# Moving a cross-partition sum of squares from TensorE to GpSimd, and packing a prefix count into fewer matmuls, in a fused scan and mixture-of-experts layer

## The chip, the cores and the metric

The kernel runs on one core of one Trainium2 chip. The metric is the device time of one execution in microseconds (us). The kernel before takes 681.78 us, the median of 3 runs (680.64 to 683.04). A difference of about 0.3% is what a measurement of this kernel can tell from none.

## What is computed

The reference, cut to what matters (8 sequences of 512 tokens, 256 features; 8 experts of 1024 hidden units, two chosen per token, and one shared expert that every token uses):

```python
xn = layernorm(x)
# scan branch
g, v, d = xn @ Wg + bg, xn @ Wv + bv, xn @ Wd + bd
a = 0.001 + 0.998 * sigmoid(d)
scan = linear_scan(sigmoid(g) * tanh(v), a)          # along each sequence
# expert branch, T = 4096 tokens
scores = sigmoid(xn @ Wgate.T + bg + bias)
weights = scores of the two best experts of a token, 0 for the others
h = gelu(einsum('td,ehd->teh', xn, W1) + b1)
combined = einsum('ted,te->td', einsum('teh,edh->ted', h, W2) + b2, weights)
shared = gelu(xn @ Ws1.T + bs1) @ Ws2.T + bs2
out = x + scan + shared + combined
```

## The kernel before, in words

All matrix products are done in float16 pairs: a float32 matrix is scaled by a power of two and split into a high and a low half, and three products (high by high, high by low, low by high) are added in PSUM. The scale of a weight matrix comes from the sum of its squares, so each of the nine weight sets (set 0 is the shared expert's, sets 1 to 8 the experts') needs that sum before it can be split.

The program has two parts. The first goes over the 8 sequences, b = 0 to 7, and does for each the layer norm, the three projections, the scan, the shared expert and the choice of experts; beside it the weight set b + 1 is loaded, measured and split into the big tile `W`. The second part goes over 43 slots of rows that were gathered by expert. The order on every engine is written out by hand: each engine has its own instruction stream in program order and waits on semaphores.

What the change and the prediction touch in the first part, for sequence b:

- **ScalarE** (`squares`, L574 to L589) squares weight set b + 1 in four pieces and leaves four sums per partition in `ssq`; the last piece (L586) raises `ssq_ok`.
- **TensorE** (`norm_sum`, L1260 to L1266) multiplies `ssq` by a matrix of twos, which adds it up over the 128 partitions and puts the result in PSUM, and raises `norm_ok`. In sequences 1 to 6 it stands behind the first second-layer step (`layer2(0)`), in 0 and 7 behind the third.
- **VectorE** (`scales`, L817 to L838) waits on `norm_ok`, works out the scales and raises `scale_ok`. It stands behind `split_wide(1)` (L940, L941: the activation of hidden block 1 is split into halves), and `split_wide(2)` stands behind it. TensorE's `layer2(2)` (L1320) waits for `split_wide(2)`.
- **ScalarE** (`high_part`, L597) waits on `scale_ok` and writes the high halves, VectorE (`low_part`, L844) the low ones.
- **TensorE** (`ranks`, L1277 to L1284) counts for every token and expert how many earlier tokens chose the same expert: a triangle matrix `before` for the token's own tile of 128 and `ones` for each earlier tile, 14 matmuls of 8 columns. VectorE (`places`) turns the counts into places in the lists and raises `place_ok`.
- **GpSimd** writes the lists with 8 indirect transfers per sequence (`scatter`, L499). Their instructions are spread out, each behind an event of ScalarE. It also does a power for the layer norm (`rstd`, L478, L480). Its queue in a sequence b is: scatters 4 to 6 of b - 1, `rstd(b + 1)`, scatter 7 of b - 1, two small copies (`fill_entries`, L489), scatters 0 to 3 of b. For the last sequence all 8 scatters of b = 7 stand at the end.
- **SyncE** waits for all list transfers, loads the first slots' lists, GpSimd gathers their rows, and TensorE transposes them (`row_transposes`, L1390): this is how the second part begins.

```python
for b in range(SEQS):
    for c in range(4, 7):
        if b: scatter(b - 1, c)
    if b + 1 < SEQS: rstd(b + 1)
    if b: scatter(b - 1, 7)
    if b + 1 < SEQS: fill_entries(b + 1)
    for c in range(4 if b + 1 < SEQS else 8): scatter(b, c)
```

Of the kernel before, what the change touches and what calls it, by code (L numbers as in the profile page):

```python
# [29 lines left out]
ALU, ACT, AX = mybir.AluOpType, mybir.ActivationFunctionType, mybir.AxisListType  # L30
RMAX, RADD = bass.bass_isa.ReduceOp.max, bass.bass_isa.ReduceOp.add

P = 128
SEQS, SEQ, D, H, E = 8, 512, 256, 1024, 8
TOKENS = SEQS * SEQ
TPB = SEQ // P
# [87 lines left out]
def layer(nc, x, w1, w2, gates, b1, b2, gbias, sbias, out):  # L124
    ctx = ExitStack()
    with ctx:
# [90 lines left out]
        ones_i, lows_i = onesf[:, 66:74].bitcast(I32), onesf[:, 74:82].bitcast(I32)  # L217
        item_sets, item_addr, item_used = (bs2[:, 193 + i * TAIL:193 + (i + 1) * TAIL] for i in range(3))
        scratch = small[:, 172:173]
        carry, ebase = small[:, 176:184], small[:, 184:192]  # L220
        one = small[:, 192:200]
        top_z = small[:, 200:208].rearrange("p (k t) -> p k t", k=2)
# [232 lines left out]
        def _(pool):  # L455
# [20 lines left out]
            def rstd(b):  # L476
                pool.wait_ge(var_ok, b + 1)
                made(pool.tensor_tensor(out=rs, in0=ve, in1=neghalf, op=ALU.pow))  # L478
                own.settle()
                pool.tensor_tensor(out=shift, in0=shift, in1=rs, op=ALU.mult).then_inc(rs_ok, 1)  # L480
# [10 lines left out]
            def scatter(b, c):  # L491
# [5 lines left out]
                else:  # L497
# [2 lines left out]
                    list_dram, bass.IndirectOffsetOnAxis(ap=place[u][:, c:c + 1], axis=0),  # L500
                    entry[u][:, 2 * c:2 * c + 2], None).then_inc(list_out[u], 16)

            rstd(0)
            made(pool.iota(spare.rearrange("p (r c) -> p r c", c=2)[:, :, 0], pattern=[[1, ROWS]], base=TOKENS,
                           channel_multiplier=0))
# [15 lines left out]
            for b in range(SEQS):  # L521
                for c in range(4, 7):
                    if b:
                        scatter(b - 1, c)
                if b + 1 < SEQS:
                    rstd(b + 1)
                if b:
                    scatter(b - 1, 7)
                if b + 1 < SEQS:
                    fill_entries(b + 1)  # L530
                for c in range(4 if b + 1 < SEQS else 8):
                    scatter(b, c)
# [275 lines left out]
        def _(dve):  # L808
# [8 lines left out]
            def scales(n):  # L817

                dve.wait_ge(norm_ok, 1 if n is None else n + 2)
                sums = ps_y[0][:, 0:2] if n is None or isinstance(n, int) and n == 0 else ps_l[:, 128:130]  # L820
                if isinstance(n, int) and n == 0:
                    dve.wait_ge(b1_red, 1)
                root_i, pw_i, scl_i = root.bitcast(I32), pw[:, 2:3].bitcast(I32), scl.bitcast(I32)
                seq(V.tensor_scalar(total.bitcast(I32), sums.bitcast(I32), SMALLEST, 0.5, ALU.max, ALU.mult))
                seq(V.tensor_scalar(root_i, total.bitcast(I32), EXPONENT, None, ALU.bitwise_and))
                own.mark(V.tensor_scalar(scl_i[:, 0:2], root_i, -1.0, float((268 - 63) << 23), ALU.mult, ALU.add))
                if n is None:
                    own.mark(V.tensor_scalar(a_gate, root[:, 0:1], 2.0 ** 63 / (TOP * XSCALE), None, ALU.mult))
                    V.tensor_scalar(a_half, root[:, 0:1], 2.0 ** 62 / (TOP * XSCALE), None,
                                    ALU.mult).then_inc(scale_ok, 1)  # L830
                    return
                set_ = PT[:, bass.ds(n, 1), :].squeeze(1)
                seq(V.tensor_scalar(bound, root[:, 0:1], 2.0 ** 68, b1red[:, bass.ds(n, 1)], ALU.mult, ALU.add))
                own.mark(V.tensor_scalar(set_[:, 0:1], root[:, 0:1], 2.0 ** 63 / (TOP * XSCALE), None, ALU.mult))
                seq(V.tensor_scalar(pw_i, bound.bitcast(I32), EXPONENT, None, ALU.bitwise_and))
                own.mark(V.tensor_scalar(set_[:, 1:2].bitcast(I32), pw_i, -1.0, float(268 << 23), ALU.mult, ALU.add))
                V.tensor_scalar(set_[:, 2:3], root[:, 1:2], 2.0 ** 63 / TOP ** 2, pw[:, 2:3], ALU.mult,
                                ALU.mult).then_inc(scale_ok, 1)  # L838
# [408 lines left out]
        def _(pe):  # L1247
# [17 lines left out]
                    ins = T.matmul(sums, onesf[:, :], halves[:, :, part], start=part == 0, stop=part == 1)  # L1265
                ins.then_inc(norm_ok, 1)  # L1266

            def logits(b, u):
                pe.wait_ge(xT_ok, b * 2 + 2)
                for t in range(TPB):  # L1270
                    for n in range(3 * KD):
                        c, (xp, wp) = n // 3, PASSES[n % 3]
                        ins = T.matmul(ps_l[:, t * E:(t + 1) * E], xT[u][:, 2 * xp + c, t * P:(t + 1) * P],
                                       gw[:, wp, c, GATES:GCOL], start=n == 0, stop=n == 3 * KD - 1)
                ins.then_inc(logit_ps, 1)

            def ranks(b):  # L1277

                pe.wait_ge(top_ok, b + 1)
                for t in range(TPB + 1):  # L1280
                    for v in range(min(t + 1, TPB)):
                        ins = T.matmul(ps_l[:, 64 + t * E:64 + (t + 1) * E], (before if v == t else ones)[:, :],
                                       mask[:, v * E:(v + 1) * E], start=v == 0, stop=v == min(t, TPB - 1))
                ins.then_inc(rank_ps, 1)  # L1284

            def scan_transposes(b, i):
# [108 lines left out]
                return pe.snap(w * WSET)  # L1395

            def sequence(b, u, first=False, last_=False):
                logits(b, u)
                for k in range(PROJ + AHEAD):
                    if k == PROJ and first:  # L1400
                        for part in range(2):
# [6 lines left out]
                for i in range(KH):  # L1408
                    if i + AHEAD < KH:
                        make(b, u, PROJ + i + AHEAD)  # L1410
                    if i == KH - 1 and last_:
                        pe.wait_ge(route_ok, 1)
                        pe.wait_ge(r_ok, b * 2 + 2)
                        row_transposes(order(0))
                    if i == 0:
                        pe.wait_ge(y_ok, b * 2 + 2)
                        if first:
                            for part in range(2):
                                pe.wait_ge(stage_used[1][part], 1)
                    pe.wait_ge(hhl_ok, b * KH + i + 1 + RING)  # L1420
                    layer2(hhlw[i % WIDE], ps_y, i, None)
                    if i == (2 if first or last_ else 0):
                        pe.wait_ge(place_ok, b + 1)
                        norm_sum(b + 1, ps_l[:, 128:130])
                    if i == 1:
                        pe.wait_ge(scan_ok, b * 2 + 2)
                        scan_transposes(b, 0)
                    if i == 2:
                        pe.wait_ge(r_ok, b * 2 + 1)
                        scan_transposes(b, 1)  # L1430
                    if i == 4 + first and not last_:
                        pe.wait_ge(xhl_ok, b + 2)
                        pe.wait_ge(r_ok, b * 2 + 2)
                        x_transposes(b + 1, 0)
                    if i == 5 + first and not last_:
                        pe.wait_ge(xT_ok, b * 2 + 3)
                        x_transposes(b + 1, 1)
# [92 lines left out]
```

## Time and profile before

| what | value |
|---|---|
| median of 3 runs | 681.78 us (680.64 to 683.04) |
| the profiled execution: its time | 678.43 us |
| the profiled execution: its span | 676.6 us |
| mean granted TensorE clock in it | 0.994 of full |
| TensorE busy | 642.1 us (95%), 6246 instructions |
| VectorE busy | 513.3 us (76%) |
| ScalarE busy | 435.6 us (64%) |
| GpSimd busy | 281.4 us (42%), 263 instructions |
| first part (all of the gate and list work) | to about 284 us of the span |

The span is the time between the first and the last instruction that the profiler saw; the execution's own time has 1.83 us more around it. Durations below come from this one execution, so sums are made against 678.43 us; the median of the runs is 3.35 us above it. An engine's share of busy time is a mean over the span; whether an engine is the bound is read stretch by stretch.

### The profile page before, as it was taken

What the parts mean: (1) busy time and instruction counts of PE and PEld (TensorE: products, weight loads), DVE (VectorE), ACT (ScalarE), POOL (GpSimd) and SP (SyncE); (2) the same over time, 40 slices, a digit from 0 to 9 for tenths busy, and PEclk for the clock granted to TensorE, in tenths of its full rate; (3) what the DMA queues carried; (4) which work ended last, traced back from release to release, by engine and by line L of the source; (5) the groups of instructions that cost most, each with busy time, mean ns of one, the idle gap of its engine ahead of it and who ended that gap; (6) DMA issues with size and microseconds to landing.
All of it is one profiled execution on the core that took longest, in us unless ns stands there. A gap on an engine that the chain in (4) does not pass through costs nothing.

```text
span 676.6 us, 19821 instructions
## 1 busy us (share of the span) xinstructions
PE 642.1 (95%) x6246; PEld 505.7 (75%) x6247; DVE 513.3 (76%) x1328; ACT 435.6 (64%) x774; POOL 281.4 (42%) x263
## 2 busy tenths in 40 slices
PE   4899999999999999799999999999999999999993
PEld 3465757575656666588888888888888888888893
DVE  4899899999999989878666666666667667666772
ACT  6987786969696965455555545565566565656562
POOL 2133333324241515634454535344454636354432
PEclk9999999999999999999999999999999999999997
DMA  7525344342525141423333345355655666575622
GB/s 244 203 52 168 95 126 100 119 128 90 154 86 164 63 122 36 129 54 52 69 55 63 55 117 169 63 126 135 173 168 147 175 159 191 143 180 148 193 33 29
DMA packets 63264, 80.77 MB, mean 119 GB/s; under 512 B 19492, under 2 KB 55268, under 8 KB 60376
## 3 DMA queue, kind: packets, MB, share of 16 engines
q1 hardware_dynamic: 48072, 62.08, 28.8%
q0 software_dynamic: 15120, 17.77, 15.6%
q8 instruction: 40, 0.66, 0.4%
q14 instruction: 32, 0.26, 0.1%
HBM read 38.66 MB, written 18.10 MB: 84 GB/s over the span
## 4 chain that ended last, share of the span: by engine, by line
PE 79%; DVE 9%; issue 5%; ACT 3%; DMA 3%; DVEq 1%; POOL 0%; POOLq 0%; SPq 0%; ACTq 0%
PE bank L1320 30%; PE bank L1312 29%; PE bank L1300 7%; PE bank L1348 4%; PE bank L1371 3%; PE bank L1390 2%; DVE arena L941 2%; DVE arena L940 2%; DVE W L844 1%; ACT arena L641 1%; PE bank L1291 1%; DMA arena<-in_gates 1%; DVE arena L883 1%; PE bank L1256 1%; DMA out<-arena,slot_adds 1%
## 5 line engine op out<-in xcount | busy, mean ns | idle before, releaser
L1320 PE MATMUL bank<-W,arena 128*128 (+1 forms) x2112 | 277.1, 273 | 5.4 <-DVE arena L941 4.9
L1312 PE MATMUL bank<-rows,W 128*128 128x256 f16 (+1 forms) x1728 | 272.7, 296 | 4.7 <-issue 3.0
L641 ACT ACTIVATE arena<-bank,par 128x256 f32<-128x256 f32 (+2 forms) x344 | 164.5, 516 | 111.3 <-PE bank L1312 74.4
L1320 PEld LDWEIGHTS bank<-W,arena 128*128 128x128 f16 x2112 | 200.9, 98 | 42.1 <-issue 6.9
L1312 PEld LDWEIGHTS bank<-rows,W 128*128 (+1 forms) x1728 | 164.8, 98 | 58.9 <-issue 7.9
L555 POOL DMA_INDIRECT out<-arena,slot_adds x71 | 115.3, 1624 | 186.7 <-ACT arena L766 130.6
L940 DVE TENSOR_SCALAR arena<-arena,par 128x256 f16<-128x256 f32 (+1 forms) x284 | 102.3, 360 | 57.6 <-ACT arena L641 46.4
L941 DVE SCALAR_TENSOR_TENSOR arena<-arena,par 128x256 f16<-128x256 f32 (+1 forms) x284 | 133.9, 472 | 10.0
L499 POOL DMA_INDIRECT lists<-entry,place x64 | 70.6, 1103 | 125.1 <-ACT arena L623 66.5
L1300 PE MATMUL bank<-rows,W 128*128 128x512 f16 x288 | 63.8, 379 | 0.0
L647 ACT ACTIVATE rows<-bank 128x1024 f16<-128x1024 f16 (+2 forms) x43 | 36.1, 840 | 37.5 <-PE bank L1390 24.9
L623 ACT ACTIVATE arena<-bank,small 128x512 f32<-128x512 f32 x48 | 36.8, 772 | 30.8 <-PE bank L1300 27.7
L630 ACT ACTIVATE arena<-bank,PT 128x512 f32<-128x512 f32 x64 | 49.2, 771 | 11.2 <-DVE arena L941 11.2
L1300 PEld LDWEIGHTS bank<-rows,W 128*128 128x128 f16 x288 | 27.5, 98 | 31.7
L941 DVE SCALAR_TENSOR_TENSOR arena<-arena,PT 128x512 f16<-128x512 f32 x64 | 48.3, 754 | 2.3
L542 POOL DMA_INDIRECT rows<-xhl_rows,slot_rows x37 | 40.1, 1083 | 18.9 <-issue 12.0
L844 DVE SCALAR_TENSOR_TENSOR W<-stage,small,W 128x1024 f16<-128x1024 f32 (+1 forms) x32 | 39.9, 1278 | 0.8 <-ACT W L597 0.8
L542 POOL DMA_INDIRECT arena<-xhl_rows,slot_rows x34 | 35.8, 1054 | 10.4 <-issue 9.8
L766 ACT ACTIVATE arena<-arena,slot_adds 128x256 f32<-128x256 f32 x56 | 25.3, 500 | 18.6 <-DVE arena L1202 17.3
L940 DVE TENSOR_SCALAR arena<-arena,PT 128x512 f16<-128x512 f32 x64 | 31.1, 486 | 8.0 <-PE bank L1320 5.1
L597 ACT ACTIVATE W<-stage,small 128x1024 f32 (+1 forms) x32 | 36.4, 1140 | 0.0
L586 ACT ACTIVATE W<-stage 128x1024 f32 (+1 forms) x32 | 33.4, 1046 | 0.0
(189 smaller groups left out, 574.7 us busy)
## 6 DMA issues: line engine op xcount, KB each, us to landing
stage<-in_w SPq DMA_DIRECT2D x32, 512.0 KB
stage<-W SPq DMA_DIRECT2D x14, 1024.0 KB
arena<-W SPq DMA_DIRECT2D x8, 1024.0 KB
arena<-in_x SPq DMA_DIRECT2D x8, 512.0 KB
xhl_rows<-W SPq DMA_DIRECT2D x8, 512.0 KB, 3.7
out<-arena SPq DMA_DIRECT2D x8, 512.0 KB
b2row<-in_b SPq DMA_DIRECT2D x22, 128.0 KB
arena<-in_b SPq DMA_DIRECT2D x21, 128.0 KB
```

Of the source, the lines that this page charges most:

```text
L499: pool.indirect_dma_start(list_dram, bass.IndirectOffsetOnAxis(ap=place[u][:, c:c + 1], axis=0), entry[u][:, 2 * c:2 * c + 2], None).then_ ...
L542: pool.indirect_dma_start(xg[s.c][0:s.parts, t, :], None, xhl_dram, bass.IndirectOffsetOnAxis(ap=slot_rows[s.c][0:s.parts, t, 0:1], axis=0 ...
L555: pool.indirect_dma_start(out, bass.IndirectOffsetOnAxis(ap=slot_adds[s.c][0:s.parts, t, 0:1], axis=0), y_sb[s.u][0:s.parts, t * D:(t + 1) ...
L623: A((sg[ch], tv[ch], dec)[g], ps_e[(2 * u + i) % RING][:, :], ACT.Tanh, bias=sbt[:, 2 * g + ch:2 * g + ch + 1], scale=(a_half, a_gate, a_h ...
L630: A(h32w[i % WIDE], ps_e[(2 * u + PROJ + i) % RING][:, :], ACT.Gelu, bias=PT[:, 0, 4 + i:5 + i], scale=PT[:, 0, 0:1]).then_inc(ev_act, 1)
L641: ins = A(h32[k][:, c], ps_e[k][:, c], ACT.Gelu, bias=p[:, 4 + e * i + jj:5 + e * i + jj], scale=p[:, 0:1])
L844: ins = V.scalar_tensor_tensor(out=W[:, bass.ds(o + HALF, HALF // 2)], in0=landing(n, l)[:, part * HALF // 2:(part + 1) * HALF // 2], scal ...
L940: seq(V.tensor_scalar(hi, v, p[:, 1:2], None, ALU.mult))
L941: V.scalar_tensor_tensor(out=lo, in0=v, scalar=p[:, 1:2], in1=hi, op0=ALU.mult, op1=ALU.subtract).then_inc(hhl_ok, 1)
L1300: ins = T.matmul(ps_e[(2 * u + i) % RING][:, :], gw[:, wp, c, o:o + P], xT[u][:, 2 * xp + c, :], start=n == 0, stop=n == 3 * KD - 1)
L1312: ins = T.matmul(bank_, weights(w, wp * HALF + c * H + j * P, P), rhs[:, 2 * xp + c, :], start=n == 0, stop=n == 3 * KD - 1)
L1320: ins = T.matmul(banks[t // 2][:, (t % 2) * D:(t % 2 + 1) * D], h[:, hp, t * P:(t + 1) * P], weights(w, (2 + wp) * HALF + j * D, D), start ...
```

## The change

The sums over partitions for sets 2 to 8 (seven calls, the third to the ninth by count from 1) move from TensorE to GpSimd: an all-reduce of the four partial sums, then two small `tensor_tensor` additions (the second doubles the sum, as the matrix of twos did). Sets 0 and 1 stay on TensorE. `scales` reads the GpSimd result from SBUF for n from 2 on. TensorE's wait on `place_ok` moves from `norm_sum` to the start of the next sequence's `logits`. `ranks` becomes 5 matmuls of up to 32 columns that accumulate into shifted windows of one PSUM region.

```diff
@@ names
+        norm4, norm2 = small[:, 240:244], small[:, 244:246]
@@ gpsimd
+            def norm_sum(n):
+
+                pool.wait_ge(ssq_ok, n + 2)
+                made(pool.partition_all_reduce(norm4, ssq, P, RADD))
+                own.settle()
+                halves = norm4.rearrange("p (l q) -> p l q", q=2)
+                made(pool.tensor_tensor(out=norm2, in0=halves[:, :, 0], in1=halves[:, :, 1], op=ALU.add))
+                own.settle()
+                pool.tensor_tensor(out=norm2, in0=norm2, in1=norm2, op=ALU.add).then_inc(norm_ok, 1)
+
...
                 if b:
                     scatter(b - 1, 7)
+                if b:
+                    norm_sum(b + 1)
                 if b + 1 < SEQS:
                     fill_entries(b + 1)
@@ vector, scales
-                sums = ps_y[0][:, 0:2] if n is None or isinstance(n, int) and n == 0 else ps_l[:, 128:130]
+                sums = norm2
+                if n is None or isinstance(n, int) and n == 0:
+                    sums = ps_y[0][:, 0:2]
+                elif isinstance(n, int) and n == 1:
+                    sums = ps_l[:, 128:130]
@@ tensor
-            def logits(b, u):
+            def logits(b, u, first):
                 pe.wait_ge(xT_ok, b * 2 + 2)
+                if not first:
+                    pe.wait_ge(place_ok, b)
...
-                for t in range(TPB + 1):
-                    for v in range(min(t + 1, TPB)):
-                        ins = T.matmul(ps_l[:, 64 + t * E:64 + (t + 1) * E], (before if v == t else ones)[:, :],
-                                       mask[:, v * E:(v + 1) * E], start=v == 0, stop=v == min(t, TPB - 1))
+                for v in range(TPB + 1):
+                    n = min(TPB + 1 - v, TPB) * E
+                    ins = T.matmul(ps_l[:, 64 + v * E:64 + v * E + n], (ones if v else before)[:, :], mask[:, 0:n],
+                                   start=v == 0, stop=v == TPB, skip_group_check=True)
...
-                    if i == (2 if first or last_ else 0):
+                    if i == 2 and first:
                         pe.wait_ge(place_ok, b + 1)
                         norm_sum(b + 1, ps_l[:, 128:130])
```

GpSimd's queue in one of the sequences 1 to 6, before: scatters 1 to 6 of the sequence before, `rstd`, scatter 7, the copies of `fill_entries`. (`small` holds the statistics, `rt` the routing tables, `entry` and `place` what a scatter writes and where.)

```order
L499 DMA lists<-entry,place 33792x2 [waits ev_act] x6
L478 TENSOR_TENSOR small<-small 128x4 [waits var_ok]
L480 TENSOR_TENSOR rt<-rt,small 128x4 [waits pool_own]
L499 DMA lists<-entry,place 33792x2 [waits ev_act]
L489 COPY entry<-token 128x4 [waits list_out1]
```

```order
L479 TENSOR_TENSOR small<-small 128x4 [waits var_ok]
L481 TENSOR_TENSOR rt<-rt,small 128x4 [waits pool_own]
L500 DMA lists<-entry,place 33792x2 [waits ev_act]
L507 ISA
L507 ISA small<-small 128x4 [waits ssq_ok]
L510 ISA
L510 TENSOR_TENSOR small<-small 128x2 [waits pool_own]
L512 TENSOR_TENSOR small<-small 128x2 [waits pool_own]
L490 COPY entry<-token 128x4 [waits list_out1]
```

Five instructions stand between scatter 7 and the copies, two of them changes of library: one before the all-reduce, one before the additions. This piece stands in the program seven times.

GpSimd's queue in the last sequence, before: scatter 7 of sequence 6 is in the row of seven, and the eight of sequence 7 follow.

```order
L489 COPY entry<-token 128x4 [waits list_out1]
L489 COPY entry<-token 128x4
L499 DMA lists<-entry,place 33792x2 [waits place_ok,entry_ok]
L499 DMA lists<-entry,place 33792x2 [waits ev_act] x7
```

And now:

```order
L500 DMA lists<-entry,place 33792x2 [waits ev_act] x7
L507 ISA
L507 ISA small<-small 128x4 [waits ssq_ok]
L510 ISA
L510 TENSOR_TENSOR small<-small 128x2 [waits pool_own]
L512 TENSOR_TENSOR small<-small 128x2 [waits pool_own]
L500 DMA lists<-entry,place 33792x2 [waits place_ok,entry_ok]
```

The eight scatters of sequence 7 now stand behind the all-reduce's wait on `ssq_ok`, the sum of squares of set 8.

TensorE's `ranks` now (L1301; `before` and `ones` are the matrices, `rt` holds the mask); before, 14 matmuls 128x8 stood there:

```order
L1319 MATMUL bank<-rows,W 128x512 x5
L1298 REGISTER_ALU
L1301 MATMUL bank<-rt,before 128x32 [waits top_ok]
L1301 MATMUL bank<-rt,ones 128x32
L1301 MATMUL bank<-rt,ones 128x24
L1301 MATMUL bank<-rt,ones 128x16
L1301 MATMUL bank<-rt,ones 128x8
```

It keeps its place behind the last projection and in front of the first hidden blocks.

## Rows read from the trace of the kernel before

**Rows 1.** Stretch (sequence 4): length, busy PE, PEld, DVE, ACT, POOL, clock, DMA, GB/s

```profile
148.40:180.20 31.80, 31.80 (x251) 20.53 (x248) 29.19 (x70) 24.96 (x37) 10.57 (x12) 1.00 0.36 116
```

**Rows 2.** Timeline of TensorE in sequence 4: start, us, operation [idle before, releaser]

```profile
163.48 0.51 PE L1265 MATMUL bank<-small,onesf 128*128 128x2 f32 x4
163.85 1.46 PE L1312 MATMUL bank<-rows,W 128*128 128x512 f16 x6
...
168.18 1.47 PE L1320 MATMUL bank<-W,arena 128*128 128x256 f16 x12
```

**Rows 3.** Timeline of VectorE in sequence 4, scales and the split behind it

```profile
164.92 0.15 DVE L824 TENSOR_SCALAR small<-bank 128x2 int32<-128x2 int32 x1
...
166.32 0.21 DVE L837 TENSOR_SCALAR PT<-small 128x1 f32 x1
...
167.04 0.75 DVE L941 SCALAR_TENSOR_TENSOR arena<-arena,PT 128x512 f16<-128x512 f32 x1
```

**Rows 4.** Timeline of TensorE in sequence 5, ranks: the first, and what follows them

```profile
188.48 0.17 PE L1282 MATMUL bank<-rt,before 128*128 128x8 f16 x1
...
188.83 0.38 PE L1312 MATMUL bank<-rows,W 128*128 128x512 f16 x1
```

**Rows 5.** Timeline of GpSimd in sequence 4, scatter 7

```profile
162.11 1.03 POOL L499 DMA_INDIRECT lists<-entry,place  x1 [0.16 <-issue]
```

**Rows 6.** Timeline of ScalarE in sequence 4, the end of the last squares

```profile
162.58 0.19 ACT L586 ACTIVATION_READ_ACCUMULATOR W<-stage 128x1 f32 x1
```

**Rows 7.** Library changes on GpSimd, by line: durations in ns, first and last start

```profile
L471 POOLq MODIFY_POOL_CONFIG  x2: 11/11/11, 1.8 to 1.9; - x2
L471 POOL TENSOR_SCALAR_AFFINE_SELECT ident<-ident x1: 290/290/290, 1.9 to 1.9; 128x128 f16<-128x128 f16 x1
L519 POOLq MODIFY_POOL_CONFIG  x2: 8/8/8, 10.6 to 10.6; - x2
L478 POOLq MODIFY_POOL_CONFIG  x2: 100/100/100, 20.0 to 20.1; - x2
L480 POOL TENSOR_TENSOR rt<-rt,small x8: 200/202/447, 8.2 to 225.5; 128x4 f32<-128x4 f32 x8
```

**Rows 8.** Timeline of GpSimd near the start: the all-reduce and what follows

```profile
19.65 0.42 POOL L519 PARTITION_ALL_REDUCE small<-small  x1 [9.05 <-issue]
26.84 1.68 POOL L478 TENSOR_TENSOR small<-small 128x4 f32<-128x4 f32 x1 [6.76 <-DMA out<-arena]
```

**Rows 9.** Timeline of VectorE near the start: what the all-reduce waits for, who waits for it

```profile
15.01 0.22 DVE L1162 TENSOR_REDUCE small<-PT 128x9 f32<-128x72 f32 x1
...
20.18 0.16 DVE L824 TENSOR_SCALAR small<-bank 128x2 int32<-128x2 int32 x1 [0.87 <-POOL small L519]
```

**Rows 10.** Timeline of ScalarE in sequence 7, the end of the last squares

```profile
259.89 0.20 ACT L586 ACTIVATION_READ_ACCUMULATOR W<-stage 128x1 f32 x1
```

**Rows 11.** Timeline of GpSimd in sequence 7: scatter 7 of sequence 6; scatters 6, 7 of sequence 7

```profile
246.97 0.96 POOL L499 DMA_INDIRECT lists<-entry,place  x1 [6.38 <-ACT arena L623]
...
262.72 0.96 POOL L499 DMA_INDIRECT lists<-entry,place  x1 [0.30 <-issue]
263.98 0.96 POOL L499 DMA_INDIRECT lists<-entry,place  x1 [0.30 <-ACT arena L630]
```

**Rows 12.** The chain that ended last, at the end of the first part: start, us, what

```profile
263.98 3.46 DMA lists<-entry,place
...
269.02 1.99 DMA slot_rows<-lists
```

**Rows 13.** Timeline of TensorE where the second part begins

```profile
276.49 0.61 PE L1390 MATMUL bank<-ident,rows 128*128 128x128 f16 x8 [1.46 <-DMA rows<-xhl_rows,slot_rows]
```

**Rows 14.** Timeline of TensorE at the end of the program: its last matmuls

```profile
665.80 0.84 PE L1371 MATMUL bank<-W,arena 128*128 x6 [0.83 <-DVE arena L941]
```

**Rows 15.** Stretches behind its last matmul, columns as in rows 1: the granted clock

```profile
668.00:669.00 1.00, 0.00 (x0) 0.00 (x0) 0.00 (x0) 0.00 (x0) 0.00 (x0) 0.98 0.75 68
669.00:670.00 1.00, 0.00 (x0) 0.00 (x0) 0.00 (x0) 0.00 (x0) 0.00 (x0) 0.50 0.42 64
```

More of the change, by code:

```diff
@@ L1397, in sequence @@
             def sequence(b, u, first=False, last_=False):
-                logits(b, u)
+                logits(b, u, first)
                 for k in range(PROJ + AHEAD):
```

## The prediction, made before the change was run

> **What bounds the kernel now.** I looked first at busy time by stretch. In a sequence of the first part TensorE is busy for all 31.80 us and VectorE for 29.19, GpSimd for 10.57 [rows 1]. So TensorE is the bound there, VectorE is close behind it, and GpSimd has two thirds of its time free. What an engine off the bound costs is then a question of who waits for it, so I read the timelines around the seven places that change, with sequence 4 as the example (sequences 1 to 6 have the same order), then the end of the first part, then the one all-reduce that GpSimd already does.
>
> In sequence 4 scatter 7 ends at 163.14 [rows 5], the last squares of the new weight set at 162.77 [rows 6]. TensorE's sum runs at 163.48 [rows 2]. VectorE starts `scales` at 164.92, ends it at 166.53, and ends the split of block 2 at 167.79 [rows 3]. TensorE starts `layer2(2)`, which needs that split, at 168.18 [rows 2]. From the start of `scales` to the moment when `layer2(2)` could run are 2.87 us, so the sum may be ready as late as 168.18 - 2.87 = 165.31 before TensorE stands still. Counted from the end of scatter 7, where the new GpSimd work begins, GpSimd has **2.17 us** for everything that it now does there.
>
> **What TensorE saves.** The sum costs it 163.85 - 163.48 = 0.37 us [rows 2], seven times: 2.6 us. The 14 rank matmuls take 188.83 - 188.48 = 0.35 us, 25 ns each [rows 4]; nine fewer, in 8 sequences, are 9 x 25 ns x 8 = 1.8 us (a matmul of 32 columns I price like one of 8; at twice that, 0.8 us of the 1.8 remains). At most 4.4 us, if nothing else holds the sequence.
>
> **What GpSimd gets.** Per call: the gap behind a scatter, 0.30 us [rows 11]; the all-reduce, 0.42 [rows 8], for 9 columns where it will have 4; two additions at 0.20 [rows 7]; three hand-overs by semaphore at about 0.1 (20.07 to 20.18 from the all-reduce to VectorE [rows 8, 9]). Together **1.4 us**, which fits into 2.17. Without anything else the change is free for VectorE, and saves TensorE time.
>
> The rest is the two changes of code library. For the first library at the start of the program nothing is paid: change at 1.8 to 1.9, the next operation at 1.9 [rows 7]; it was already there. For the all-reduce's library it is different: the change is at 10.6 [rows 7], its semaphore came from VectorE's reduction, which ends at 15.23 [rows 9], yet it starts at 19.65, and the page names no other wait [rows 8]. VectorE waited for it [rows 9]. So 19.65 - 15.23 = **4.42 us** behind the wait, or 19.65 - 10.6 = 9.05 us from the change, went into loading. The way back is at 20.0 [rows 7] and the next `tensor_tensor` at 26.84, released by a transfer [rows 8]: the load back took between 0 and 26.84 - 20.1 = 6.74 us, hidden by that transfer. The trace has no second change to this library, so whether a repeated one is cheaper is not shown. Per call, then: between 0 and 9.05 for the way there, between 0 and 6.74 for the way back. I take 4.42 for each: the one load that is seen, for two changes of the same kind, L = 8.84 in all. In the new order the wait for `ssq_ok` is already over when scatter 7 ends (162.77 against 163.14), so nothing covers the load.
>
> The Trainium skill (GPSIMD Engine Reference, section 2.1, Instruction dispatch) says that the first call to a freshly loaded kernel pays about 6 us for the load (5.95), counted as the gap behind `MODIFY_POOL_CONFIG` less the wait on the event. This trace gives 4.42 by the same count. With 5.95 for each way, an estimate from that page of the Trainium skill, the time below would be 777 us in place of 756.
>
> **The sum.** *Sequences 1 to 6.* With L = 8.84 the sum is ready 1.4 + 8.84 = 10.24 us behind scatter 7, and TensorE's `layer2(2)` is 10.24 - 2.17 = 8.1 us late. TensorE's queue is in order, so nothing behind it can move up; `split_wide(2)` and the rest of VectorE's queue stand behind `scales`, ScalarE's `high_part` waits for `scale_ok`, and the list scatters 0 to 3 stand behind the sum on GpSimd (10.6 + 10.2 of some 40 us: it keeps up). TensorE has no idle time later in a sequence to win it back [rows 1]. The margin of sequence 4 stands for all six: 6 x 8.1 = **48.4 us**. What TensorE saved lies ahead of the stall and goes into it; I credit nothing.
>
> *Sequence 7.* The sum of set 8 now stands ahead of the eight scatters of sequence 7. Its squares end at 260.09 [rows 10]; the first scatter could begin at 260.09 + 1.1 (the 1.4 without the gap) + 0.3 and the last one, seven spacings of 1.26 later [rows 11], at 270.3, against 263.98 before [rows 11]: 6.3 us late even if loading cost nothing. Nothing covers that: the last list write and the loads behind it are on the chain that ended last [rows 12], and TensorE already stood idle for 1.46 us for the rows that follow from it [rows 13]. With L behind the wait it is 6.3 + 8.84 = **15.1 us**. That `scales` for set 8 is also late lies beside it.
>
> *The clock.* TensorE's last matmul ends at 666.64 [rows 14]; the granted clock is still 0.98 in the stretch up to 669 and 0.50 behind it [rows 15]: a TensorE that stands still falls from 2.4 to 1.2 GHz, and stalls of 8 us may do the same. No row shows it come back, so the price is open: 0, or one step of the second layer taken at half speed behind each stall, 1.47 us more [rows 2], or two such. I take one, seven times: **10.3 us**.
>
> The new wait of `logits` on `place_ok` costs nothing: the matmuls that waited on the same count ran at 163.48 [rows 2], 17 us ahead of the next `logits`. Reading the sum from SBUF in place of PSUM changes one 0.15 us operation [rows 3].
>
> Sum: 48.4 + 15.1 + 10.3 = 73.8. On the profiled execution 678.43 + 73.8 = 752.2; the median of the runs lies 3.35 above that execution, so **755.6 us**, some 11% slower. Within this case the clock alone moves it between 745 and 766.
>
> **Rivals.**
> 1. *Repeated changes of library cost nothing* (the code stays once it is loaded; the change does in effect not reload). For: the change at 1.9 us cost nothing [rows 7], and the trace has no second load. Against: the one load that is seen cost 4.42 us. Then the sequences lose nothing and TensorE keeps up to 4.4 us, but the tail of sequence 7 gives 6.3 back: 678.43 + 6.3 - 4.4 = 680.3, as a median **683.7 us**, +0.3%.
> 2. *Faster.* The same, and the tail is covered. The place is TensorE's wait for the first gathered rows [rows 13]. It decides as soon as the two loads together stay under 2.17 - 1.4 = 0.8 us and the last list write lands in time, for which the eight scatters would have to issue in about a third of their spacing. Price: 681.78 - 4.4 = **677.4 us**. The rows speak against both halves.
> 3. *Only the way there is paid*, 4.42, because the first library stays. 6 x (5.82 - 2.17) = 21.9, tail 6.3 + 4.42 = 10.7, clock half of the above for stalls less than half as long, 5: 37.6, so **719 us**. For: the first change at 1.9 us. Against: then the all-reduce's library would not need to be loaded again either.
> 4. *Loads as long as the bounds allow*, 9.05 from the change and 6.74 back. 6 x (1.4 + 15.79 - 2.17) = 90.1; in the tail the change at 247.9 [rows 11] is done by 257, before the squares, so 6.3 + 6.74 = 13.0; clock 10.3: 113.4, so **795 us**. For: the trace cannot exclude it. Against: with the DMA queues quieter than at the start, a load should not be longer there.
>
> **How the numbers follow.** Both loads paid at about the seen price: 0.45. Rival 1: 0.16, 3: 0.18, 4: 0.15, 2: 0.06. A difference under 0.3% is what a measurement of this kernel can't tell from none. Rival 1 sits at that edge: of its 0.16, 0.05 are slower, 0.10 the same and 0.01 faster. So faster 0.07, same 0.10, slower 0.83. The range runs from 683 (rival 2 and half of rival 1 left out, 0.14) to 797 (what lies above rival 4 left out, about 0.06). The main case by itself is 740 to 772.
>
> **What would show it.** In the profile after: seven more all-reduces, each several us behind the end of scatter 7 and of the squares; idle time of VectorE ahead of `scales` (its first operation) of about 8 us each, released by GpSimd's last addition; TensorE idle ahead of `layer2(2)`; a sequence of about 40 us; a granted clock below 1 behind those stalls; the last list scatter of sequence 7 some 15 us later against the squares of set 8. It is wrong if the second all-reduce starts within 1 us of scatter 7's end, or if the addition follows the all-reduce at once: then rival 1 or 3 holds. If VectorE waits and TensorE doesn't, the margin of 2.17 us was misread.

## The result, and the profile after

The kernel after takes **788.61 us** (median of 6 runs, 786.63 to 793.64), the kernel before beside it 682.41 (680.64 to 683.86): ratio 1.156, 95% interval 1.1535 to 1.159. The forecast was 755.6 in a range of 683 to 797, so direction and range hold and the size is 33 us short. The profiled execution took 789.35 us; its span of 787.6 stands against 676.6 before, 111.0 longer.

The head of the page after, its engines and the granted clock in 40 slices:

```profile
span 787.6 us, 19673 instructions
PE 655.6 (83%) x6146; PEld 509.6 (65%) x6147; DVE 515.3 (65%) x1328; ACT 435.7 (55%) x774; POOL 283.9 (36%) x284
PEclk9999796978969798898799999999999999999998
```

TensorE is busy for 83% of the span, and in the first half of the slices the clock dips once for each sequence.

**Where the time is.** The first matmul of `logits` marks the start of each sequence on TensorE. The trace after gives these starts, to be read against 31.80 us for a sequence before [rows 1]:

```
sequence      1      2      3       4       5       6       7     first rows
before     52.46  84.16  116.06  148.27  180.11  212.13  243.82    276.49
after      52.40  97.33  144.70  191.86  239.29  286.92  332.62    379.38
```

Sequences 1 to 6 take 280.2 us in place of 191.4 (+88.8); from sequence 7 to the first transpose of the gathered rows 46.8 in place of 32.7 (+14.1); the second part 408.2 in place of 400.1 (+8.1). These three are the whole difference.

**One stall.** The timelines of GpSimd, VectorE and TensorE in sequence 4 (start, us, operation [idle before, releaser]), to be held against [rows 2, 3, 5]:

```profile
205.82 1.03 POOL L500 DMA_INDIRECT lists<-entry,place  x1 [0.17 <-issue]
213.72 0.44 POOL L507 PARTITION_ALL_REDUCE small<-small  x1 [6.87 <-issue]
221.35 0.18 POOL L510 TENSOR_TENSOR small<-small 128x2 f32<-128x2 f32 x1 [7.19 <-issue]
221.62 0.19 POOL L512 TENSOR_TENSOR small<-small 128x2 f32<-128x2 f32 x1
```

```profile
207.81 0.75 DVE L958 SCALAR_TENSOR_TENSOR arena<-arena,PT 128x512 f16<-128x512 f32 x1
221.84 0.17 DVE L841 TENSOR_SCALAR small<-small 128x2 int32<-128x2 int32 x1 [13.28 <-POOL small L512]
...
223.98 0.75 DVE L958 SCALAR_TENSOR_TENSOR arena<-arena,PT 128x512 f16<-128x512 f32 x1
```

```profile
224.79 2.74 PE L1339 MATMUL bank<-W,arena 128*128 128x256 f16 x12 [12.95 <-DVE arena L958]
227.32 1.06 PE L1310 MATMUL bank<-identf,arena 128*128 128x128 f32 x4
228.18 2.54 PE L1331 MATMUL bank<-rows,W 128*128 128x512 f16 x6
230.55 1.47 PE L1339 MATMUL bank<-W,arena 128*128 128x256 f16 x12
```

Scatter 7 ends at 206.85. The all-reduce, whose squares were done, starts 6.87 us later, and the addition 7.19 us behind the all-reduce; "issue" says that GpSimd waited for nothing that the profile shows. Both gaps stand behind a change of library. The sum is ready 14.96 us behind scatter 7, 12.79 more than the margin of 2.17, and TensorE stands still for 12.95 us ahead of `layer2(2)`. The other five sequences read the same: stalls of 12.30, 13.79, 12.68, 12.86 and 12.61 us, with sequence 4 **77.2 us**.

Grouped by line for the whole program (count, busy, mean ns, idle before and its releaser):

```profile
L507 POOL PARTITION_ALL_REDUCE small<-small x7 | 3.1, 443 | 55.1 <-issue 43.0 <-ACT W L599 12.1
L510 POOL TENSOR_TENSOR small<-small 128x2 f32<-128x2 f32 x7 | 1.3, 183 | 49.0 <-issue 49.0
```

```profile
L841 DVE TENSOR_SCALAR small<-small 128x2 int32<-128x2 int32 x7 | 1.2, 169 | 81.3 <-POOL small L512 81.3
```

The way there takes 43.0 / 6 = 7.2 us, the way back 49.0 / 7 = 7.0: 14.2 in each call. The seventh all-reduce is the one that waited for ScalarE.

**The clock.** Stretches of 2 us around the same stall (columns as in [rows 1], the granted clock third from the end):

```profile
214.00:216.00 2.00, 0.00 (x0) 0.00 (x0) 0.00 (x0) 0.00 (x0) 0.16 (x1) 1.00 0.00 0
216.00:218.00 2.00, 0.00 (x0) 0.00 (x0) 0.00 (x0) 0.00 (x0) 0.00 (x0) 0.67 0.00 0
218.00:220.00 2.00, 0.00 (x0) 0.00 (x0) 0.00 (x0) 0.00 (x0) 0.00 (x0) 0.50 0.00 0
...
228.00:230.00 2.00, 2.00 (x7) 0.83 (x6) 1.54 (x3) 1.64 (x2) 0.00 (x0) 0.50 0.20 59
230.00:232.00 2.00, 2.00 (x16) 1.42 (x15) 1.49 (x2) 1.17 (x2) 0.12 (x1) 0.91 0.70 139
```

TensorE fell to 1.2 GHz while it stood still and was still there at 230, after it had worked since 224.79. So `layer2(2)` took 2.74 us in place of 1.47, and the transposes and matmuls behind it 1.06 and 2.54. From the start of `layer2(2)` to the next `layer2` are 5.76 us here and 3.19 before; over the six stalls 30.9 against 19.1, **11.7 us**. Stalls and clock are 88.9, which is what the six sequences lost; of TensorE's saved matmuls nothing shows.

**The end of the first part.** GpSimd's timeline in sequence 7, the last squares of set 8 on ScalarE, and TensorE's first transposes, to be held against [rows 10, 11, 13]:

```profile
335.77 0.96 POOL L500 DMA_INDIRECT lists<-entry,place  x1 [6.68 <-ACT arena L636]
348.79 0.45 POOL L507 PARTITION_ALL_REDUCE small<-small  x1 [12.06 <-ACT W L599]
355.95 0.18 POOL L510 TENSOR_TENSOR small<-small 128x2 f32<-128x2 f32 x1 [6.71 <-issue]
...
356.95 1.20 POOL L500 DMA_INDIRECT lists<-entry,place  x1 [0.54 <-issue]
...
368.11 0.96 POOL L500 DMA_INDIRECT lists<-entry,place  x1 [0.30 <-issue]
```

```profile
348.46 0.19 ACT L599 ACTIVATION_READ_ACCUMULATOR W<-stage 128x1 f32 x1
```

```profile
379.38 1.01 PE L1409 MATMUL bank<-ident,rows 128*128 128x128 f16 x8 [14.52 <-DMA rows<-xhl_rows,slot_rows]
380.19 2.77 PE L1339 MATMUL bank<-W,arena 128*128 128x256 f16 x12
```

This all-reduce starts 0.14 us behind the squares (348.65): the change stood at 337.0, and its load ran **beside the wait**. The way back costs 6.71 here too. The last scatter starts 19.5 us behind the squares, 3.9 before: 15.6 late, and TensorE's wait for the rows grew from 1.46 to 14.52. Here too it came back at 1.2 GHz: its granted clock is 0.50 from 379 to 383, and 12 matmuls take 2.77 us. The first slot of the second part lasts 12.79 us (to 392.17), in place of 10.24 before (276.49 to 286.73) and 11.40 in e3 below, where TensorE hardly waited; in e5, with the same wait, it lasts 12.82. So the clock costs an estimated 1.4 to 2.6 us at this place, and they lie in the 8.1 of the second part.

### The profile page after: what moved, and what is told of

Read it like the earlier page. It is cut to its first block, busy times and chain, and to the rows that moved or that the text cites. A ratio compares the mean times of both kernels' runs of the same rounds, so it can differ in the third digit from the quotient of the medians.

```text
span 787.6 us, 19673 instructions
## 1 busy us (share of the span) xinstructions
PE 655.6 (83%) x6146; PEld 509.6 (65%) x6147; DVE 515.3 (65%) x1328; ACT 435.7 (55%) x774; POOL 283.9 (36%) x284
## 4 chain that ended last, share of the span: by engine, by line
PE 55%; issue 18%; DVE 16%; ACT 3%; POOL 3%; another core or an unknown queue 2%; DMA 1%; DVEq 1%; POOLq 0%; ACTq 0%; SPq 0%
PE bank L1339 23%; PE bank L1331 20%; PE bank L1367 4%; DVE W L861 3%; PE bank L1390 3%; PE bank L1409 2%; DVE arena L958 2%; DVE arena L957 2%; ACT arena L654 1%; DVE arena L894 1%; DVE small L870 1%; DVE arena L913 1%; POOL small L479 1%; PE bank L1319 1%
## 5 line engine op out<-in xcount | busy, mean ns | idle before, releaser
L1339 PE MATMUL bank<-W,arena 128*128 (+1 forms) x2112 | 286.2, 279 | 89.0 <-DVE arena L958 88.6
L1339 PEld LDWEIGHTS bank<-W,arena 128*128 128x128 f16 x2112 | 204.4, 100 | 132.9 <-DVE arena L958 89.7
L1331 PE MATMUL bank<-rows,W 128*128 128x256 f16 (+1 forms) x1728 | 276.4, 299 | 3.4 <-ACT arena L654 2.2
L500 POOL DMA_INDIRECT lists<-entry,place x64 | 71.0, 1109 | 129.6 <-ACT arena L636 69.1
L643 ACT ACTIVATE arena<-bank,PT 128x512 f32<-128x512 f32 x64 | 49.2, 771 | 18.7 <-DVE arena L958 15.3
L841 DVE TENSOR_SCALAR small<-small 128x2 int32<-128x2 int32 x7 | 1.2, 169 | 81.3 <-POOL small L512 81.3
L608 ACT ACTIVATE small<-small 128x1 f32<-128x1 f32 x9 | 1.8, 203 | 84.9 <-DVE PT L854 84.9
L555 POOL DMA_INDIRECT rows<-xhl_rows,slot_rows x37 | 38.5, 1039 | 23.8 <-DMA slot_rows<-lists 12.9
L555 POOL DMA_INDIRECT arena<-xhl_rows,slot_rows x34 | 35.1, 1032 | 10.4 <-issue 10.4
```

Source lines behind the costliest of these rows:

```text
L500: pool.indirect_dma_start(list_dram, bass.IndirectOffsetOnAxis(ap=place[u][:, c:c + 1], axis=0), entry[u][:, 2 * c:2 * c + 2], None).then_ ...
L555: pool.indirect_dma_start(xg[s.c][0:s.parts, t, :], None, xhl_dram, bass.IndirectOffsetOnAxis(ap=slot_rows[s.c][0:s.parts, t, 0:1], axis=0 ...
L643: A(h32w[i % WIDE], ps_e[(2 * u + PROJ + i) % RING][:, :], ACT.Gelu, bias=PT[:, 0, 4 + i:5 + i], scale=PT[:, 0, 0:1]).then_inc(ev_act, 1)
L1331: ins = T.matmul(bank_, weights(w, wp * HALF + c * H + j * P, P), rhs[:, 2 * xp + c, :], start=n == 0, stop=n == 3 * KD - 1)
L1339: ins = T.matmul(banks[t // 2][:, (t % 2) * D:(t % 2 + 1) * D], h[:, hp, t * P:(t + 1) * P], weights(w, (2 + wp) * HALF + j * D, D), start ...
```

## The experiments

The theory: a change of library holds GpSimd for about 7 us from the change on, there and back, and what is paid of it is what someone waits for. Rivals: the handover by way of GpSimd costs by itself, or GpSimd's lateness does. "Before" below is the median of the kernel before, run beside each.

**e1: the two changes in the kernel before, with nobody waiting for a sum.**

```diff
                 if b:
                     scatter(b - 1, 7)
+                if b and b + 1 < SEQS:
+                    load the all-reduce's library
+                    load the first library
```

> The kernel before (TensorE keeps every sum), plus two changes of GpSimd's code library, there and back, behind scatter 7 of sequences 1 to 6: no operation that anyone waits for stands behind them but GpSimd's own copies and scatters. Theory: what costs time is only that VectorE's scales waits for the loads; GpSimd has 21 us of 32 free. Then 682 us, at most 686. Rival: GpSimd's own lateness (lists, the root of the next sequence) or the transfer of the code costs the time by itself: then over 700 us, near 770 if it is all of it.

Measured: 685.37, before 682.63, ratio 1.005 (1.003 to 1.007). GpSimd in sequence 4, and its copies for the whole program:

```profile
163.28 1.03 POOL L500 DMA_INDIRECT lists<-entry,place  x1 [0.17 <-issue]
178.88 0.77 POOL L490 COPY entry<-token 128x4 uint32<-128x4 uint32 x2 [14.56 <-issue]
```

```profile
L490 POOL COPY entry<-token 128x4 uint32<-128x4 uint32 x16 | 4.8, 324 | 88.3 <-issue 88.1 <-POOL rt L515 0.2
```

The two loads take 88.1 / 6 = 14.7 us, as in the kernel after (14.2), with no all-reduce between them, and they hold even the plain copy behind them. Twelve loads, 88 us of GpSimd, cost the kernel 2.7 us. So they are paid through the wait of `scales`, not by the lateness of GpSimd's own work.

**e2: all the waits and handovers, no library change.**

```diff
-                made(pool.partition_all_reduce(norm4, ssq, P, RADD))
+                made(pool.tensor_tensor(out=norm4, in0=ssq, in1=ssq, op=ALU.add))
```

> The kernel after, with each of the seven all-reduces replaced by an addition out of GpSimd's first library, at the same place, behind the same wait; the sum over the partitions is left out. No change of library is left, all the waits and hand-overs are. Theory (the loads are the cost; the 1.4 us of handwork fit into the margin of 2.17 us): the six sequences lose nothing, the end of the first part keeps its 6.3 us, TensorE saves up to 4.4: 680 to 690 us. Rival (the handover by way of GpSimd costs by itself, or the new order of the lists): 700 us or more.

Measured: 693.07, ratio 1.015 (1.012 to 1.019): 3 us above the theory's range and 7 below the rival's 700. GpSimd in sequence 4, then in sequence 7:

```profile
194.21 1.03 POOL L500 DMA_INDIRECT lists<-entry,place  x1 [0.16 <-issue]
195.28 0.78 POOL L507 TENSOR_TENSOR small<-small 128x4 f32<-128x4 f32 x1
196.13 0.36 POOL L510 TENSOR_TENSOR small<-small 128x2 f32<-128x2 f32 x1
196.57 0.71 POOL L512 TENSOR_TENSOR small<-small 128x2 f32<-128x2 f32 x1
...
260.38 0.19 POOL L507 TENSOR_TENSOR small<-small 128x4 f32<-128x4 f32 x1 [12.00 <-ACT W L599]
...
270.85 0.97 POOL L500 DMA_INDIRECT lists<-entry,place  x1 [0.30 <-issue]
```

The sum is ready 197.28 - 195.24 = 2.04 us behind scatter 7; 1.4 was forecast, and it fits into 2.17. The six sequences together take 192.1 us, before 191.4. The end of the first part takes 40.1 in place of 32.7: 7.4 us, forecast 6.3. These two are 8.1 of the 10.4 us by which e2 is slower; the rest is not explained. The loads are the cost in the sequences; without them the move still loses the end of the first part and gains nothing elsewhere.

**e3: only the eighth set back on TensorE.**

```diff
-                if b:
+                if b and b + 1 < SEQS:
                     norm_sum(b + 1)
...
-                    if i == 2 and first:
+                    if i == 2 and (first or last_):
```

> The kernel after, with the sum of the eighth weight set back on TensorE in the last sequence of the first part, so that no library is changed ahead of the last eight list scatters; the six sequences before keep GpSimd's sums. Theory: the last scatter came 15.6 us later behind the squares, TensorE began the second part 14.1 us later behind its last logits: 774 us, and if the 8 us that the second part became longer hang on that too, 766. Rival (the chain of the lists is hidden anyway): 786 to 789.

Measured: 774.13, ratio 1.134 (1.130 to 1.139), the theory's 774; 14.5 us less than the kernel after. TensorE waits 0.24 us for the first rows:

```profile
365.76 0.61 PE L1409 MATMUL bank<-ident,rows 128*128 128x128 f16 x8 [0.24 <-DMA rows<-xhl_rows,slot_rows]
```

The second part stayed long: 771.7 - 365.76 = 405.9 us. So the late lists did not make it long.

**e4: only the ranks in 5 matmuls**, on the kernel before.

> The kernel before with only the ranks in 5 matmuls in place of 14. Nine matmuls of 25 ns fewer in 8 sequences: theory, 1.8 us faster at most, 680 to 682.4 us, since ranks stands on TensorE, which has no idle time in a sequence. Rival: nothing, because the transposes behind it wait for ScalarE and VectorE anyway: 682.4 us.

Measured: 683.14, before 682.63, ratio 1.001 (0.999 to 1.003): no difference. The matmuls themselves in sequence 5, to be held against [rows 4]:

```profile
188.23 0.18 PE L1282 MATMUL bank<-rt,before 128*128 128x32 f16 x1
188.26 0.24 PE L1282 MATMUL bank<-rt,ones 128*128 128x32 f16 x4
188.36 1.46 PE L1312 MATMUL bank<-rows,W 128*128 128x512 f16 x6
```

They take 0.13 us in place of 0.35, which in 8 sequences is the 1.8 us of the forecast, and the second part did begin at 274.61 in place of 276.49. But that part took 680.8 - 274.61 = 406.2 us against 400.1, with the same instructions (404.8 in e1). It varies by more than the gain from one profiled execution to another, so the 8.1 us by which it was longer in the kernel after can't be put down to the change as a whole. The interval of the medians leaves no room for a gain of 1.8 us; where it goes is not shown.

**e5: one load ahead of `scales` in place of two.**

```diff
-                made(pool.partition_all_reduce(norm4, ssq, P, RADD))
...
-                pool.tensor_tensor(out=norm2, in0=norm2, in1=norm2, op=ALU.add).then_inc(norm_ok, 1)
+                pool.partition_all_reduce(norm4, ssq, P, RADD).then_inc(norm_ok, 1)
+                load the first library
...
+                    seq(V.tensor_tensor(norm2, halves[:, :, 0], halves[:, :, 1], ALU.add))
+                    seq(V.tensor_scalar(norm2, norm2, 2.0, None, ALU.mult))
```

> The kernel after, with the two additions moved to VectorE (two short operations ahead of scales) and the change back to the first library put right behind the all-reduce: only the way there stands ahead of scales, and the way back runs behind it, ahead of GpSimd's copies and scatters. Theory (each change takes GpSimd about 7 us from the change on, whoever waits; the sequence pays what stands ahead of scales): a stall of 0.3 + 7.1 + 0.5 + 0.5 - 2.2 = 6.2 us and 1.4 for the clock in place of 14.8, six times, so 43 less than the kernel after; the end of the first part stays, since the way back still stands ahead of the eight scatters: 745 us. If scatters can issue during the way back: 738. Rival (the loads are not what the sequence pays): 780 or more.

Measured: 752.50, ratio 1.104 (1.101 to 1.107): 36 us less than the kernel after, 43 forecast. GpSimd by line, then TensorE in sequence 6:

```profile
L508 POOL PARTITION_ALL_REDUCE small<-small x7 | 3.1, 444 | 55.0 <-issue 42.0 <-ACT W L596 13.0
L491 POOL COPY entry<-token 128x4 uint32<-128x4 uint32 x16 | 2.7, 194 | 42.1 <-issue 41.9 <-POOL rt L522 0.2
```

```profile
279.88 2.74 PE L1340 MATMUL bank<-W,arena 128*128 128x256 f16 x12 [4.99 <-DVE arena L959]
```

The way there is 42.0 / 6 = 7.0 us and still paid; the way back, 7.0, has moved to the copies, where nobody waits for it. TensorE's six stalls are 5.0 to 6.5 us (33.5 together; 6.2 each was forecast). The stall halved, but the clock's price did not: from `layer2(2)` to the next `layer2` TensorE takes 4.7 to 5.8 us in place of 3.19, 13.1 us in all, where 1.4 a stall was forecast. The way back still stands ahead of the eight scatters of sequence 7, and that end is as long as in the kernel after (47.5 us). Some 5 us of the sequences are not explained.

**e6 and e7: no change of library in the sequences.** The all-reduce stays; the two additions and the inverse root of the variances of sequences 2 to 8, which need the first library, go to VectorE. The all-reduce's library is then loaded once, at the start. e7 is e6 with the eighth sum on TensorE.

```diff
-                if b + 1 < SEQS:
-                    rstd(b + 1)
...
+                seq(V.tensor_scalar(rs.bitcast(I32), ve.bitcast(I32), -0.5, float(0x5f3759df), ALU.mult, ALU.add))
+                for _ in range(3):
+                    seq(V.scalar_tensor_tensor(out=y, in0=rs, scalar=-0.5, in1=rs, op0=ALU.mult, op1=ALU.mult))
+                    seq(V.tensor_tensor(y, y, ve, ALU.mult))
+                    seq(V.scalar_tensor_tensor(out=rs, in0=y, scalar=1.5, in1=rs, op0=ALU.add, op1=ALU.mult))
```

> The kernel after with no change of library in the sequences: the all-reduce's library stays, because the other two uses of the first one go to VectorE, the two additions (2 short operations) and the inverse root of the variances of sequences 2 to 8 (11 short operations by Newton's method in place of GpSimd's power). The all-reduce itself stays, with its wait. Theory: the six sequences lose only what VectorE's 13 short operations add (some 2 us of VectorE in a sequence that leaves it 2.6 idle: 0 to 1 us each), the end of the first part loses 7 us: 688 to 697 us. Rival (the all-reduce or the handover costs by itself): over 720.

> The kernel before the last one, with the sum of the eighth set back on TensorE: no change of library, and nothing new ahead of the last eight scatters. Theory: 682 to 690 us, the same as the kernel before or up to 1% slower by VectorE's added operations. Rival (what is left of the change, the all-reduce six times and TensorE's fewer matmuls, is worth something by itself): under 680.4.

Measured: 715.00 (ratio 1.048, 1.046 to 1.051) and 707.36 (1.036, 1.034 to 1.039). Both are slower than the theory's range; e6 is still under its rival's 720, and e7's rival, faster than before, falls. VectorE in one sequence of e6:

```profile
177.02 0.17 DVE L880 TENSOR_SCALAR small<-small 128x4 int32<-128x4 int32 x1
...
179.25 0.16 DVE L885 TENSOR_TENSOR rt<-rt,small 128x4 f32<-128x4 f32 x1
179.44 0.49 DVE L964 TENSOR_SCALAR arena<-arena,PT 128x512 f16<-128x512 f32 x1
```

The 11 operations take 2.4 us, and the split behind them starts at once: VectorE's queue has no gap there. A sequence takes some 35 us in place of 32. The 2.6 us that VectorE is idle in a sequence [rows 1] lie elsewhere in it; that was the mistake of the expectation. e6 loses 7.6 us more than e7 by the eighth sum, much as e2 lost 7.4 at that place. e8 and e9 take the 11 operations out of e7, and e10 finds another 4 us of e9.

**e8: one step of Newton's method in place of three** (6 operations fewer; the inverse root is less exact), and **e9: none of the 11** (the root of sequence 1 serves all).

> The kernel e7 with one step of Newton's method in place of three, so 6 of VectorE's 11 added operations are left out (the inverse root is then less exact). Theory: e7 is slow because VectorE's queue has no gap between its reductions and split_wide(2), so each added operation there, about 0.2 us with its gap, is paid in the seven sequences that it stands in: 6 x 0.2 x 7 = 8.4 less than 707.4, 699 us. Rival (the all-reduce with its wait is what e7 pays): 707.

> The kernel e7 without any of the 11 operations (the inverse root of the variances of sequences 2 to 8 is left out; the value of sequence 1 is used). The all-reduces on GpSimd, their waits and the two additions on VectorE remain, and no library changes. Theory: 2.4 us less in each of seven sequences than e7, 690 us, and down to 683 if the two additions (0.4 us) find a gap. Rival (the all-reduce by itself): 700 or more.

Measured: 695.64 (ratio 1.022, 1.020 to 1.024) and 688.63 (1.012, 1.008 to 1.015). The 11 operations in seven sequences cost 18.7 us, 0.24 us each, and 6 of them 11.7, where the theory had 8.4. With six all-reduces, their waits and two additions on VectorE left, sequences 2 to 5 take 32.4 to 32.5 us each, before 31.8 to 32.2. That is far too little for the 7.9 us that e9 still lies above the kernel before (680.75 beside it). Its trace shows where most of them are, at the start of the program, on GpSimd (the second line belongs to the last section):

```profile
12.50 0.28 POOL L472 TENSOR_SCALAR_AFFINE_SELECT ident<-ident 128x128 f16<-128x128 f16 x1 [10.93 <-issue]
...
22.90 0.42 POOL L525 PARTITION_ALL_REDUCE small<-small  x1 [6.09 <-issue]
```

In the kernel before, the operation of the first line starts at 1.9 us [rows 7], and `logits` of the first sequence starts at 15.37; in e9 at 21.36.

**e10: e9 with the first library loaded back once, behind the last all-reduce.**

```diff
                 if b and b + 1 < SEQS:
                     norm_sum(b + 1)
+                if b + 2 == SEQS:
+                    load the first library
```

> The kernel e9 (the inverse root of sequences 2 to 8 left out as there), with the first library loaded back once, behind the last all-reduce, where only GpSimd's copies and scatters stand behind it. In e9 GpSimd's first affine_select at the start of the program comes 10.9 us behind the operation before it, in the kernel before 0.4, and logits of the first sequence start at 21.36 in place of 15.37. Theory: GpSimd keeps the library with which the execution before it ended, so e9 pays a load at its own start; with the first library back at the end the start is as before: 6 us less than e9, 682.6 us. Rival (the start is late for another reason): 688.6.

Measured: 684.67, before 681.53, ratio 1.004 (1.002 to 1.006): 4.0 us less than e9, where 6 were forecast. The same place in its trace:

```profile
1.93 0.28 POOL L473 TENSOR_SCALAR_AFFINE_SELECT ident<-ident 128x128 f16<-128x128 f16 x1 [0.36 <-issue]
```

The first `logits` is at 15.34 again, 6.0 us earlier; the end of the first part is 0.9 us longer than in e9 (32.0 against 31.2), and the other 1.1 is not explained. So e6 to e9 ended with the all-reduce's library and each next execution paid for the first one at its start. With that removed, and the inverse root still left out, six all-reduces and their waits, in place of TensorE's sums, cost 0.4%: the all-reduce by itself is nearly free. Of the 25.9 us that e7 lost, VectorE's 11 operations are 18.7, the load at the start 4.0, and 3.1 are left, as in e10. No version ran faster than the kernel before.

## Why the prediction was right, and where its size was off

- **Which wait ends last:** right. VectorE's `scales` waited for GpSimd's addition, 81.3 us in seven waits, and TensorE ahead of `layer2(2)`; e1 and e2 tie that to the loads.
- **The margin of 2.17 us:** right. 14.96 - 2.17 = 12.79 against a stall of 12.95.
- **The handwork, 1.4 us:** small, as forecast; 2.04 measured in e2, and in the stall above 0.90 besides the two gaps.
- **The loads, "I take 4.42 for each": the step that failed.** Measured are 7.2 and 7.0 us, L = 14.2 in place of 8.84. The 4.42 was counted behind the wait for VectorE's reduction [rows 8, 9]. In sequence 7 of the kernel after the load ran beside such a wait and left 0.14 us behind it, so at the start of the program too the load had begun at the change, and 4.42 was only what was left of it. Counted from the change, these rows say 9.05, and for the way back at most 6.74, which five of the seven in the kernel after exceed (up to 7.34). With both bounds the stalls would be 6 x (1.4 + 15.79 - 2.17) = 90.1 us; measured are 77.2; the forecast was 48.4. That is rival 4, which was given 0.15: its mechanism is the one that ran (the load from the change on, in sequence 7 hidden beside the squares), with a load between the two prices. The Trainium skill (GPSIMD Engine Reference, section 2.1, Instruction dispatch) gives 5.95 us, as the gap less the wait on the event. By that count the trace shows 4.42 at the start, 0.14 in sequence 7 and about 7 where nothing is waited for: less the wait is not the load's length.
- **Repeated loads are paid each time,** 6.6 to 7.8 us there and 6.7 to 7.3 back, so rivals 1 and 2 fall; **both ways are paid,** so rival 3 falls, and e5, built as rival 3, gives 752.5 where that rival put 719. Rivals 1 and 3 leaned on the change at 1.9 us, which cost nothing [rows 7]. "It was already there" was right, but for a reason that says nothing of repeated changes: the execution before had left that library (e9, e10).
- **The end of the first part, 15.1 us:** 14.1 measured, partly by two errors that cancel. Of the loads only the way back, 6.71, stood behind the squares, where 8.84 was forecast; the additions and scatters made the last scatter late by the other 15.6 - 6.7 = 8.9, where 6.3 was forecast. The eight scatters alone took 368.11 - 356.95 = 11.16 between the first and the last, seven spacings of 1.59 in place of 1.26.
- **The clock, 10.3 us:** 11.7 in the six sequences. The step of the second layer was at half speed as forecast, and in most stalls part of the next one too. The seventh place adds 1.4 to 2.6; the forecast had 1.47 at each of seven.
- **"What TensorE saved goes into the stall; I credit nothing":** right. Even alone the ranks show no difference (e4).

On the new terms: 77.2 + 11.7 + 14.1 = 103.0 of the 106.2 us between the medians. The clock at the seventh place adds 1.4 to 2.6; the rest is not explained, and the second part varies by more.

## What to carry to other kernels

Before work is moved to GpSimd, see which code libraries the operations around it use: an all-reduce between two `tensor_tensor` costs two loads of some 7 us in each round, whatever its own 0.44 us. A load is counted from the change on, not from the end of the wait behind it; put early beside a wait, or behind the last thing that someone waits for, it can cost next to nothing. An engine's idle time in a stretch pays for added work only where its queue has a gap at that very place.

## What was not expected of the hardware

- A change of library holds all of GpSimd's queue: in e1 a plain copy and the scatters behind it stood for 14.56 us, though no all-reduce stands there.
- The clock's price does not shrink with the stall: 13.1 us for six stalls of 5.0 to 6.5 us (e5), 11.7 for six of 12.3 to 13.8. In both TensorE came back at 1.2 GHz, and its first 12 matmuls took 2.74 us in place of 1.47.
- A library stays from one execution to the next: a program that ends with another one than it begins with pays a load at its own start: 10.93 us on GpSimd, a first `logits` that is 6.0 us later, and 4.0 us of the time (e9 against e10).
- The length of a load is not constant. That of the all-reduce's library near the start of the program filled 9.05 us where it began at 10.6 [rows 7, 8], but 6.1 to 6.5 in e6 to e9, where it began at about 17 (e9: 6.09, shown above); those in the sequences of the kernel after filled 6.6 to 7.8, and the load of the first library at the start of e6 to e9 10.8 to 11.3. What sets the length was not tried.
